# Moving a layer norm's scale out of h and into the propagation matrix, in a two-layer graph network in fp32

## The reference, cut to what matters

```python
# layer 0
h = max(_layernorm(x), 0);  x = x + relu(attention(h, adj))     # this x is the kernel's x1
# layer 1
h = jnp.maximum(_layernorm(x, axis=-1), 0.0)
x = x + _L1_gnn_ref(h, adj, ...)
# in _L1_gnn_ref, on x = h:
h1 = relu(hypergraph_conv(h, adj, W1, b1));  h1 = layer_norm(h1, gamma, beta)
y  = hypergraph_conv(h1, adj, W2, b2)
return y + x                                                     # x here is h
# hypergraph_conv(x): Dn * (H @ (Be * (H^T @ (x @ W^T)))) + b
```

## Time and profile before

| | us |
|---|---|
| median of 3 executions (2589.3 to 2633.85) | 2596.53 |
| the profiled execution's own time | 2600.14 |
| its span | 2598.0 |
| PE busy | 2437.5 (94%) |
| DVE busy | 2074.0 (80%) |
| ACT busy | 1700.0 (65%) |
| POOL busy | 1407.9 (54%) |

### The profile page before, as it was taken

How to read it: one execution, slowest core, us unless ns; L and a number is a source line. 1 busy time by engine, 2 the same in 40 slices (tenths; PEclk the granted TensorE clock), 3 DMA queues, 4 the chain that set the end, 5 groups by cost and what they waited for, 6 DMA issues and landing times. The chain is left out here.

```text
span 2598.0 us, 50103 instructions
## 1 busy us (share of the span) xinstructions
PE 2437.5 (94%) x13972; PEld 2095.4 (81%) x13972; DVE 2074.0 (80%) x4256; ACT 1700.0 (65%) x4361; POOL 1407.9 (54%) x1684
## 2 busy tenths in 40 slices
PE   3799999999999999999999999999999999999997
PEld 2688888888888888888888888888888888888885
DVE  4877888888888888888888888887888888888884
ACT  2566666666666666666666666766666666666663
POOL 3565555555555555555555555555555555555543
PEclk9799999999999999999999999999999999999999
DMA  5345444444444444444444444445444444444432
GB/s 189 83 135 137 127 132 133 123 136 135 126 134 134 121 139 134 120 139 134 120 139 131 123 136 138 121 139 136 124 133 131 124 134 131 129 128 136 130 106 69
DMA packets 656392, 336.14 MB, mean 129 GB/s; under 512 B 554608, under 2 KB 570992, under 8 KB 656368
## 3 DMA queue, kind: packets, MB, share of 16 engines
q1 hardware_dynamic: 638512, 303.35, 41.6%
q10 hardware_dynamic: 17856, 32.51, 3.6%
HBM read 234.50 MB, written 101.26 MB: 129 GB/s over the span
## 5 line engine op out<-in xcount | busy, mean ns | idle before, releaser
L370 POOL TENSOR_TENSOR u<-u,mask 128x1024 f32<-128x1024 f32 x128 | 307.9, 2405 | 743.5 <-DMA u<-en_rows 743.5
L462 ACT ACTIVATE att<-u,shifts 128x128 f32<-128x128 f32 x1024 | 402.0, 393 | 296.1 <-DVE shifts L775 292.3
L877 PE MATMUL p_w1a<-W_hi,rT_hi 128*128 128x512 f32 x1024 | 417.7, 408 | 1.5 <-ACT rT_hi L580 1.5
L878 PE MATMUL p_w1a<-W_lo,rT_hi 128*128 128x512 f32 x1024 | 404.3, 395 | 0.0
L463 ACT ACTIVATE att_low<-u,shifts 128x128 f32<-128x128 f32 x1024 | 399.3, 390 | 0.0
L647 DVE TENSOR_TENSOR att<-att,att_low 128x512 f32<-128x512 f32 x256 | 189.0, 738 | 142.6 <-POOL nb L362 137.6
L882 PE MATMUL p_w1a<-W_hi,rT_lo 128*128 128x512 f32 x1024 | 259.6, 395 | 0.0
L766 DVE TENSOR_REDUCE neg_max<-u 128x8 f32<-128x1024 f32 x128 | 156.1, 1220 | 119.9 <-POOL u L370 119.9
L951 PE MATMUL p_att<-feats,attT 128*128 128x65 f32 x2048 | 244.4, 273 | 5.4 <-ACT attT L507 5.4
L951 PEld LDWEIGHTS p_att<-feats,attT 128*128 128x128 f32 x2048 | 240.8, 192 | 6.4 <-ACT attT L507 6.4
L981 PE MATMUL p_w1b<-G,h 128*128 128x128 f32 x1024 | 148.6, 289 | 98.1 <-ACT h L556 97.8
(11 more groups left out here) (123 smaller groups left out, 6821.0 us busy)
## 6 DMA issues: line engine op xcount, KB each, us to landing
u<-en_rows SPq DMA_DIRECT2D x130, 576.0 KB, 3.5
r_blocks<-raw SPq DMA_DIRECT2D x128, 512.0 KB, 2.6
raw<-r_blocks SPq DMA_DIRECT2D x512, 128.0 KB, 2.9
xT_in<-in_xT SPq DMA_DIRECT2D x128, 256.0 KB, 4.0
out<-raw SPq DMA_DIRECT2D x128, 256.0 KB, 2.0
x_in<-in_x ACTq DMA_DIRECT2D x124, 256.0 KB, 3.6
adj_in<-in_adj SPq DMA_DIRECT2D x128, 128.0 KB, 2.1
en_rows<-eT SPq DMA_DIRECT2D x520, 1.1 KB
```

The lines of the kernel that those rows point to most:

```text
L370: nc.gpsimd.tensor_tensor(u[:, g.slot(2), 0:HEADS, :], u[:, g.slot(2), 0:HEADS, :], mask[:, :].unsqueeze(1).broadcast_to([P, HEADS, N]), A ...
L462: nc.scalar.activation(att[:, i, :], u[:, g.slot(2), i, :], ACT.Exp, bias=shifts[:, 0, i:i + 1])
L877: mm(dst, hi, w_hi, start=first, stop=False)
L878: mm(dst, hi, w_lo, start=False, stop=False)
```

## The change

The scale leaves `h`. `h` becomes relu(x1 - mean) and needs `nm1` alone; `nb1` and the POOL instruction that made it are gone. DVE gets a new instruction that scales the rows of `G` by `rs1` into `G_rs` (128 x 128), placed after L812 and before `larger`; PE multiplies `h` by `G_rs` instead of `G`. The residual needs the scaled `h`, so ACT gets a new instruction that copies `h` times `rs1` into `rest`, a turn later, between `ve2` (L538) and the exponentials of graph t+2; POOL then adds `x1` to `rest`. POOL also gets a wait in front of that addition: for `shifts` of graph t+2. `larger` no longer waits for `nb1`, but stands behind `G_rs`, which waits for `rs1`.

```diff
--- before.py
+++ after.py
@@ -119,7 +119,8 @@
         dev = raw[:, 3, DH:2 * DH]
         ve0, ve1, ve2 = sb("ve0", [P, 1]), sb("ve1", [P, 1]), sb("ve2", [P, 1])
         rs0, rs1, rs2 = sb("rs0", [P, 4]), sb("rs1", [P, 1]), sb("rs2", [P, 2])
-        nm1, nb1 = sb("nm1", [P, 1]), sb("nb1", [P, 1])
+        nm1 = sb("nm1", [P, 1])
+        G_rs = sb("G_rs", [P, N])
         xT_in = sb("xT_in", [P, 2, DC, N])
         xc = sb("xc", [P, DC, N])
         h0 = sb("h0", [P, DC, 2, N], F32R)
@@ -182,7 +183,7 @@
 
         s_inc, s_sizes, s_row, s_cnt1, s_inv0, s_inv, s_beT, s_G, s_G_sb = (sem("s_" + n) for n in ("inc", "sizes", "row", "cnt1", "inv0", "inv", "beT", "G", "G_sb"))
 
-        s_stats1, s_mv1, s_ve1, s_rs1, s_nm1, s_nb1, s_h, s_xh, s_rest = (sem("s_" + n) for n in ("stats1", "mv1", "ve1", "rs1", "nm1", "nb1", "h", "xh", "rest"))
+        s_stats1, s_mv1, s_ve1, s_rs1, s_nm1, s_G_rs, s_h, s_hs, s_xh, s_rest = (sem("s_" + n) for n in ("stats1", "mv1", "ve1", "rs1", "nm1", "G_rs", "h", "hs", "xh", "rest"))
         s_hg, s_hg_hi, s_hg_lo, s_w1, s_pre, s_r = (sem("s_" + n) for n in ("hg", "hg_hi", "hg_lo", "w1", "pre", "r"))
         s_nm2a, s_nm2, s_sq2, s_ve2, s_rs2, s_rB, s_rB_out, s_rT, s_rT_hi, s_rT_lo = (sem("s_" + n) for n in ("nm2a", "nm2", "sq2", "ve2", "rs2", "rB", "rB_out", "rT", "rT_hi", "rT_lo"))
         s_w2, s_z, s_z_hi, s_z_lo, s_y, s_y_sb = (sem("s_" + n) for n in ("w2", "z", "z_hi", "z_lo", "y", "y_sb"))
@@ -355,12 +356,6 @@
                 pool.wait_ge(s_ve, g.count())
                 nc.gpsimd.tensor_tensor(rs, ve[:, :], halfpow[:, :], ALU.pow).then_inc(s_rs, 1)
 
-            def shift(g, nm, rs, nb, s_nm, s_rs, s_nb):
-
-                pool.wait_ge(s_nm, g.count())
-                pool.wait_ge(s_rs, g.count())
-                nc.gpsimd.tensor_tensor(nb[:, :], nm[:, :], rs[:, :], ALU.mult).then_inc(s_nb, 1)
-
             def turn(t):
                 g = t.plus(2)
                 if g.within(NG):
@@ -387,9 +382,11 @@
                     nc.gpsimd.tensor_tensor(rs2[:, g.slot(2):g.slot(2) + 1], ve2[:, :], halfpow[:, :], ALU.pow).then_inc(s_rs2, 1)
 
                     s, s4 = g.slot(2), g.slot(4)
-                    pool.wait_ge(s_h, g.count())
+                    if g.plus(2).within(NG):
+                        pool.wait_ge(s_shifts, g.plus(2).count())
+                    pool.wait_ge(s_hs, g.count())
                     pool.wait_ge(s_x1, g.count())
-                    nc.gpsimd.tensor_tensor(rest[s4], x1[:, s, :], h[:, s, :], ALU.add).then_inc(s_xh, 1)
+                    nc.gpsimd.tensor_tensor(rest[s4], x1[:, s, :], rest[s4], ALU.add).then_inc(s_xh, 1)
                     if g.base == 0:
                         pool.wait_ge(s_small, SMALL * 16)
                     pool.wait_ge(s_xh, g.count())
@@ -397,10 +394,10 @@
                 g = t.plus(1)
                 if g.within(NG):
                     if g.has(1):
-                        pool.wait_ge(s_h, g.count(1))
+                        pool.wait_ge(s_G_rs, g.count(1))
+                        pool.wait_ge(s_hs, g.count(1))
                     pool.wait_ge(s_ve1, g.count())
                     nc.gpsimd.tensor_tensor(rs1[:, :], ve1[:, :], halfpow[:, :], ALU.pow).then_inc(s_rs1, 1)
-                    shift(g, nm1, rs1, nb1, s_nm1, s_rs1, s_nb1)
                 g = t.plus(2)
                 if g.within(NG):
 
@@ -536,6 +533,12 @@
                     if g.has(1):
                         act.wait_ge(s_rs2, g.count(1))
                     nc.scalar.activation(ve2[:, :], sq2[:, :], ACT.Identity, bias=eps[:, :], scale=1.0 / DH).then_inc(s_ve2, 1)
+                g = t
+                if g.within(NG):
+
+                    act.wait_ge(s_rs1, g.count())
+                    act.wait_ge(s_h, g.count())
+                    nc.scalar.activation(rest[g.slot(4)], h[:, g.slot(2), :], ACT.Copy, scale=rs1[:, :]).then_inc(s_hs, 1)
                 if t.plus(2).within(NG):
 
                     exps(t.plus(2), 0)
@@ -548,13 +551,12 @@
                 g = t.plus(1)
                 if g.within(NG):
 
-                    act.wait_ge(s_nb1, g.count())
+                    act.wait_ge(s_nm1, g.count())
                     if g.has(2):
 
                         act.wait_ge(s_hg, g.count(2))
                         act.wait_ge(s_xh, g.count(2))
-                    nc.scalar.activation(h[:, g.slot(2), :], x1[:, g.slot(2), :], ACT.Relu, bias=nb1[:, :],
-                                         scale=rs1[:, :]).then_inc(s_h, 1)
+                    nc.scalar.activation(h[:, g.slot(2), :], x1[:, g.slot(2), :], ACT.Relu, bias=nm1[:, :]).then_inc(s_h, 1)
                     if g.base == 0:
                         rounded(3)
                 g = t.plus(-1)
@@ -807,16 +809,20 @@
                     nc.vector.bn_aggr(mv1[:, :], st1[:, :]).then_inc(s_mv1, 1)
                     dve.wait_ge(s_mv1, g.count())
                     if g.has(1):
-                        dve.wait_ge(s_nb1, g.count(1))
+                        dve.wait_ge(s_rs1, g.count(1))
+                        dve.wait_ge(s_h, g.count(1))
                     nc.vector.tensor_scalar(ve1[:, :], mv1[:, 1:2], EPS, None, ALU.add).then_inc(s_ve1, 1)
                     nc.vector.tensor_scalar(nm1[:, :], mv1[:, 0:1], -1.0, None, ALU.mult).then_inc(s_nm1, 1)
+                    dve.wait_ge(s_G_sb, g.count())
+                    if g.has(1):
+                        dve.wait_ge(s_hg, g.count(1))
+                    dve.wait_ge(s_rs1, g.count())
+                    nc.vector.tensor_scalar(G_rs[:, :], G[:, g.slot(4), 0:N], rs1[:, :], None, ALU.mult).then_inc(s_G_rs, 1)
                 if t.base == -1:
                     dve.wait_ge(k_mean_sb, 2)
                     centre(0)
                     centre(1)
                 if t.plus(2).within(NG):
-                    if t.plus(1).within(NG):
-                        dve.wait_ge(s_nb1, t.plus(1).count())
                     larger(t.plus(2), 0)
                 g = t.plus(-1)
                 if g.within(NG):
@@ -974,11 +980,11 @@
                 if g.within(NG):
 
                     pe.wait_ge(s_h, g.count())
-                    pe.wait_ge(s_G_sb, g.count())
+                    pe.wait_ge(s_G_rs, g.count())
                     if g.has(1):
                         pe.wait_ge(s_pre, g.count(1, per=2))
                     for c in range(DC):
-                        last = mm(p_w1b[:, c * P:(c + 1) * P], h[:, g.slot(2), c * P:(c + 1) * P], G[:, g.slot(4), 0:N],
+                        last = mm(p_w1b[:, c * P:(c + 1) * P], h[:, g.slot(2), c * P:(c + 1) * P], G_rs[:, :],
                                   start=True, stop=True)
                     last.then_inc(s_hg, 1)
                 g = t.plus(3)
```

## The result

The changed kernel takes 2493.39 us (median of 4, 2489.1 to 2494.4). Its ratio to the kernel before is 0.9613, 95% interval 0.9583 to 0.9643: 3.9% faster. Beside it the kernel before took 2589.3, 2596.53, 2633.85 and 2635.2 us; the ratio leaves out the two longer ones, which are over 1.5% above the shortest and count as slow executions. Beside the experiments its medians are 2614 to 2635, so their ratios can't be set against 0.9613: compare an experiment's time with 2493.39 us, and small differences with care, since they were taken on several occasions. What can be said of the scatter comes at the end.

What follows compares the result with a forecast made beforehand. The ring, not PE, was taken as the bound. At 13.36 + 4.1 = 17.5 us it would fall below PE's floor of 18.70, saving PE's waits: 2596.5 - 106.5 = 2490 us, range 2478 to 2522.

Steps and rivals of the forecast that it cites:

- the ring: Closed chain once per turn from `shifts` through L981, `eT`, HBM and L370 to the next `shifts`: 19.53 us, forecast 17.5.
- POOL's addition held L775: POOL's first residual addition (L392) keeps DVE's L775 at 1.36 us instead of 0.17; the wait saves 1.19.
- its floor: Length of a turn in which PE waits for nothing: 18.70 us.
- S to H: From S, the start of `shifts` (L775), to H, the start of L981: 6.17 us when held, forecast 4.1.
- The step that failed: From L981's start to the next turn's `shifts` start: 13.36 us, none of it touched by the change.
- the reserve of the ring: Margin by which the ring after the change, 17.5 us, would lie below PE's floor of 18.70: 1.2 us.
- the scale's move: Scale taken out of `h` into `G_rs`: L981 starts 0.9 us sooner than in a turn without the hold on L775.
- the ring scatters: Rival: POOL's trips for `u` vary and eat the reserve, 21 us stay, 2510 us; chance 0.13.
- `G_rs` or L803 is held: Rival: POOL holds DVE's `G_rs` by 1.19 us, perhaps L803 by 0.43: 2490 to 2538 us; chance 0.08.
- the detour over POOL is only moved: Rival: L981 still waits for POOL's `rs1`, at one remove: 2545 to 2600 us; chance 0.09, within 2%.
- The additions that are held until 2.6: Rival: DVE's stream from L782 to L803 keeps POOL's additions out, kernel slower, up to 2690 us; chance 0.04.
- The ACT copy: ACT's copy into `rest` before the exponentials: at most 0.82 us, covered by 1.1 to 1.4 us of waiting for `shifts`.

Runs made afterwards that it cites:

- the doses: POOL power instructions (0.55 us each) added before `rs1`: one in the kernel before, 2645.03 us; one, two, three in the changed kernel, 2544.91, 2608.16, 2681.22 us.
- the kernel before with fewer products: Kernel before, leaving out seven of PE's eight products of the low part of `rT` with the high part of W2: 2660.74 us, ratio 1.0175.
- the wait alone: Kernel before plus only POOL's wait for `shifts` of graph t+2: 2510.25 us, ratio 0.9548.
- the scale alone: Changed kernel without POOL's wait for `shifts`; also called the scale-only kernel: 2520.1 us, ratio 0.9579.
- the changed kernel with fewer products: Changed kernel, leaving out seven of PE's eight products of the low part of `rT` with the high part of W2: 2473.29 us, ratio 0.9458.

## Why the prediction was right, and where it was not

*The time.* 2490 was forecast, 2493.39 measured, in the range. The reading that carried it held: the ring and not PE set the pace (the doses, and the kernel before with fewer products), POOL's addition held L775 for 1.19 us (the wait alone), PE is at its floor after the change (it no longer waits for `h`, and its turns have a median of 18.60 us). The floor of 18.70 was read off one turn; the shortest turns are 18.59.

*The terms of S to H.* `h` ends at 4.04, forecast 4.0. The additions end at 2.92, forecast 3.0. `rs1` starts 3.39 after S, forecast 3.1 to 3.3: L803 is held by the second addition after all, for 0.17 us, where I had taken nothing and given 0.43 as the bound. The row that I took against this hold says nothing against it: in the earlier trace rows L803 ends at 1308.88 and L396 at 1308.84, so it may have been held there too, for the little that was left. The wait brings this price: the median of this instruction is 342 ns with the wait alone and 161 with the scale alone.

`G_rs` takes 0.31 and not 0.22, and the trace speaks for a hold until `beT` ends. In 125 of the 128 turns it starts 0.17 us after `beT`, takes 0.315 and ends 0.08 after `beT`'s end. In two others it starts 0.14 after `beT` and takes 0.342, or 0.05 after `G_lo` and takes 0.490, and ends 0.08 after the POOL instruction both times. L647 at that place before does the same: it starts 0.17 after `beT` and takes 0.775, or 0.08 after it and takes 0.864, and ends 0.545 after `beT`'s end in both cases. So the hold lasts as long as `beT` does, and is cheap only because 0.17 of its 0.40 us are over by then.

By the Trainium skill (SBUF — State Buffer, "SBUF: two separate sides") a DVE instruction with two SBUF inputs and a GpSimd instruction that reads SBUF lock each other out until the first is done; the rows of L805 agree, since its end, 2.94, lies on the addition's end, 2.92. With one SBUF input, L794 (0.69) and the statistics beside the same additions are not lengthened.

So H could be at 4.5, against my 4.1, a small miss; it is 4.50 on average where PE does not delay it, in the changed kernel with fewer products.

*The step that failed* is this one: "From H to the next S are 1286.21 - 1272.85 = 13.36 us, and the change touches none of it." H and the next S are that far apart, but they are not linked by way of H alone. In the kernel before, too, `hg_hi` starts just when `z_hi` makes room:

```profile
1272.77 0.74 DVE L828 SCALAR_TENSOR_TENSOR raw<-p_w1a,rs,t_bc 128x512 f32<-128x512 f32 x1
...
1273.54 0.63 ACT L566 ACTIVATE z_hi<-raw 128x512 fp32r<-128x512 f32 x1 [0.74 <-DVE raw L828]
...
1274.08 0.58 ACT L573 ACTIVATE hg_hi<-p_w1b 128x512 fp32r<-128x512 f32 x1
```

The product of `h` (1272.85 + 1.16 = 1274.01) and `z_hi` were done within a tenth of a microsecond of each other. There I had one path in view where there were two of one length. The change shortened the first much and the second little. By the averages, the product is done 6.36 us after S with the wait alone and at 5.64 in the changed kernel with fewer products; `z_hi` starts at 5.88 and at 5.67. So the reserve of the ring was 1.2 us in the prediction and 0.05 to 0.14 in the kernel. The time came out right nevertheless, because the hold alone was worth more than PE's wait. That the ring ended under PE's floor at all was luck: it did by about a tenth of a microsecond, and not by the reserve that I had counted on. Had it ended 0.2 us higher, as with the wait alone, the time would have been some 17 us longer, still in the range.

*What the scale's move brings, then.* Not 0.9 us. Against the wait alone it takes 6.43 - 6.21 = 0.2 us off the ring: `nb1` with its trip and the hold on `larger` go, `G_rs` comes. That is what lifts the kernel with the wait alone from 2510 to 2493, 17 us of the 103 between 2596.53 and 2493.39. The wait brings the rest.

*The rivals.* That the ring scatters is true in its mechanism and small in its size: 18.67 against 18.60. That `G_rs` or L803 is held is true, but by 0.1 and 0.17 only. That the detour over POOL is only moved came close: `rs1` was 0.1 to 0.3 late, which cost nothing, but the 1.2 us of reserve that I set against this rival weren't there, and 0.55 us more on POOL cost 52 us. The additions that are held until 2.6, which would have made the kernel slower, are not: they start 0.25 after S. The ACT copy is covered, twice over.

## What to carry to other kernels

When an instruction of a few elements takes as long as a large one on the engine beside it, compare their ends: a hold by a shared port shows as equal ends, and a wait that lets the small one go first can be worth more than any work removed. When two short chains on two engines start from one event and meet at such a port within hundredths of a microsecond, the order is a lottery, and an edit elsewhere can change the time by changing the odds; put the order in by a semaphore before measuring anything else.

Before counting on a reserve in a ring, ask at every station what stands in front of it on its own engine, not only what it waits for. A station that starts exactly when its predecessor ends has a second path through it, which no wait names. A dose of useless work measures the reserve in one run.

## What the runs showed of the hardware that I had not expected

**Less work for PE made the kernel slower.** The kernel before without the seven products takes 1.0175 times as long. PE in time order, and the stretches of 2 us around its wait (PEclk is the granted clock, in shares of full speed):

```profile
1211.37 0.29 PE L873 MATMUL p_fa<-W_hi,h 128*128 128x272 f32 x1
1214.04 0.58 PE L981 MATMUL p_w1b<-G,h 128*128 128x128 f32 x1 [2.38 <-ACT h L556]
```

```profile
core 0: us, PE busy (x) PEld busy (x) DVE busy (x) ACT busy (x) POOL busy (x), PEclk, DMA share, GB/s
1212.00:1214.00 2.00, 0.00 (x0) 0.00 (x0) 0.91 (x4) 0.81 (x1) 1.60 (x4) 0.94 0.92 267
1214.00:1216.00 2.00, 1.96 (x9) 1.96 (x10) 1.30 (x3) 0.63 (x1) 1.01 (x3) 0.50 0.34 118
1216.00:1218.00 2.00, 2.00 (x13) 1.99 (x13) 1.01 (x4) 1.55 (x3) 0.90 (x2) 0.70 0.00 0
```

PE stood still for 2.4 us, waiting for `h`, and then got half the clock, 1.2 GHz, for about the next 3 us (0.50 in the second stretch, 0.70 in the third). The first matmul afterwards is L981, which lies in the ring: 0.58 us for one instead of 0.38. The trace has 48 such stretches of half clock between 120 and 2470 us, where the kernel before has none, and the mean granted clock is 0.955, against 0.991. ACT, which hardly ever waited for that product in front of `hg_hi` (2.2 us, once), now does in a third of the turns:

```profile
PE p_w1b L981 <- ACT h L556: 271.0, 127, 4.2
...
ACT hg_hi L573 <- PE p_w1b L981: 34.8, 44, 2.2
```

So the products that were left out did no harm when they were there: they kept PE from standing still too long. A held turn of the kernel with fewer products is 20.4 us on average, one of the kernel before 19.7. In the changed kernel without the same products PE waits 1.2 us per turn and the granted clock is 0.991; with the wait alone it waits 194.4 / 127 = 1.5 us, and there are 8 such stretches.

**DVE holds POOL as well.** POOL's copy of a single column, L412, had a median of 648 ns and ran beside L647 of the earlier trace rows. After the change it is L409. First before, then after:

```profile
L412 POOL COPY beT<-adj_in x128: 186/648/654, 49.1 to 2544.2; 128x1 f32<-128x1 f32 x128
```

```profile
L409 POOL COPY beT<-adj_in x128: 184/185/189, 50.3 to 2437.2; 128x1 f32<-128x1 f32 x128
```

It now gets in ahead of `larger`, and `G_lo` behind it takes the hold instead (a median of 0.88 us where it was 0.45). The sum of the two is nearly the same, 1.06 us against 1.10, and no one waits for it.

**What stays open.** The scatter of the kernel before fits the lottery: all turns held instead of 80% would be at most 0.2 x 1.19 x 127 = 30 us more. None of its longer executions has a profile here, so this is argued and not shown. Nor is it known what sets the odds, a third of the turns held in the scale-only kernel and four fifths before. The addition's recorded start lies 0.027 us behind L775's there and 0.019 before (medians), which goes the right way, but by less than it scatters.
